# Attention scores in fp32 on four 32-row groups of TensorE, with the causal mask of the row maxima added on VectorE

## The reference

```python
q = jnp.einsum('btc,hcd->bhtd', x, Wq) + bq[None, :, None, :]     # 16 heads, D = 16
k = jnp.einsum('btc,hcd->bhtd', x, Wk) + bk[None, :, None, :]
v = jnp.einsum('btc,hcd->bhtd', x, Wv) + bv[None, :, None, :]
scores = jnp.einsum('bhtd,bhsd->bhts', q, k) * scale
causal = jnp.triu(jnp.full((Tn, Tn), neg, dtype=scores.dtype), k=1)
probs = jax.nn.softmax(scores + causal, axis=-1)
y = jnp.einsum('bhts,bhsd->bhtd', probs, v)
...
return y @ Wo + bo
# layer 1: no biases, q = _apply_rope(q, sin, cos), k = _apply_rope(k, sin, cos)
```

## Time and profile before

| | |
|---|---|
| time, median of 3 runs | 1030.9 us (1030.26 to 1034.15) |
| span of the profiled execution | 1058.4 us |
| PE busy | 754.7 us (71%) |
| DVE busy | 494.6 us (47%) |
| ACT busy | 330.7 us (31%) |
| POOL busy | 336.4 us (32%) |
| mean granted TensorE clock | 0.863 |

### The profile page before, as it was taken

How to read it: one execution, slowest core, us unless ns; L and a number is a source line. 1 busy time by engine, 2 the same in 40 slices (tenths; PEclk the granted TensorE clock), 3 DMA queues, 4 the chain that set the end, 5 groups by cost and what they waited for, 6 DMA issues and landing times.

```text
span 1058.4 us, 14617 instructions
## 1 busy us (share of the span) xinstructions
PE 754.7 (71%) x4353; PEld 439.7 (42%) x4353; DVE 494.6 (47%) x1442; ACT 330.7 (31%) x660; POOL 336.4 (32%) x371
## 2 busy tenths in 40 slices
PE   0930899996753889999881632589998496899970
PEld 0510334423521667666660321134434443576650
DVE  7211977804630344444444762587742740144444
ACT  1500366682200222222220340246674320032221
POOL 6210011120075255555457150001110047035560
PEclk9965899999575899999995776799999598899995
DMA  2599053480052799999997099300000111089974
GB/s 74 60 115 103 2 167 103 147 264 1 1 177 77 227 246 261 270 260 262 247 231 212 2 118 119 40 12 2 2 1 22 67 48 41 24 235 264 263 178 129
DMA packets 88634, 134.28 MB, mean 127 GB/s; under 512 B 9883, under 2 KB 67082, under 8 KB 88464
## 3 DMA queue, kind: packets, MB, share of 16 engines
q1 hardware_dynamic: 57808, 101.31, 38.0%
q0 software_dynamic: 16896, 19.37, 10.6%
q10 hardware_dynamic: 13888, 13.06, 4.4%
HBM read 80.74 MB, written 40.06 MB: 114 GB/s over the span
## 4 chain that ended last, share of the span: by engine, by line
PE 29%; DVE 18%; POOL 14%; issue 14%; DMA 11%; another core or an unknown queue 5%; SPq 4%; ACT 4%; POOLq 0%; ACTq 0%; DVEq 0%
POOL acc L578 12%; DVE mx L1134 7%; DMA KA<-X 6%; PE ps L703 5%; PE ps L687 5%; PE ps L764 4%; SPq L410 4%; PE ps L658 4%; DMA acc<-X,token 3%; PE ps L798 2%; PE ps L605 2%; POOL pause L576 2%; ACT X L922 1%; PE ps L732 1%
## 5 line engine op out<-in xcount | busy, mean ns | idle before, releaser
L1134 DVE TENSOR_REDUCE mx<-ps 128x1 f32<-128x512 f32 (+3 forms) x304 | 180.2, 657 | 128.1 <-PE ps L661 76.7
L658 PE MATMUL ps<-KA,QA 112*128 112x512 bf16 (+3 forms) x384 | 116.7, 355 | 85.6 <-ACT mT L941 44.1
L922 ACT ACTIVATE X<-ps 128x1024 f32<-128x1024 f32 (+1 forms) x192 | 146.2, 811 | 84.9 <-PE ps L687 84.3
L578 POOL DMA_INDIRECT acc<-X,token x96 | 149.8, 1561 | 15.1 <-issue 14.9
L821 PE MATMUL ps<-X,KA 128*128 128x128 f32 x1152 | 149.3, 280 | 1.4 <-DMA KA<-in_ex 0.8
L821 PEld LDWEIGHTS ps<-X,KA 128*128 128x128 f32 x1152 | 139.6, 196 | 4.3 <-issue 2.9
L555 POOL TENSOR_SCALAR_AFFINE_SELECT X<-X 128x512 f32<-128x512 f32 x64 | 40.8, 637 | 311.2 <-ACT X L922 311.2
L1337 DVE TENSOR_SCALAR X<-ps,egate 128x256 f32<-128x256 f32 x96 | 46.5, 484 | 145.5 <-DMA acc<-X,token 145.0
L566 POOL DMA_INDIRECT slot_rows<-xn,slot_i x64 | 64.8, 1013 | 127.2 <-issue 73.7
L658 PEld LDWEIGHTS ps<-KA,QA 112*128 112x128 bf16 x384 | 37.4, 103 | 157.4 <-DVE mx L1134 50.8
L990 ACT ACTIVATE X<-ps 128x256 f32<-128x256 f32 x96 | 36.9, 385 | 201.9 <-DVE token L1311 84.2
(11 more groups left out here) (174 smaller groups left out, 934.3 us busy)
## 6 DMA issues: line engine op xcount, KB each, us to landing
KA<-in_ex SPq DMA_DIRECT2D x96, 512.0 KB
slot_rows<-empty SPq DMA_DIRECT2D x12, 1060.0 KB, 10.1
X<-slot_rows ACTq DMA_DIRECT2D x96, 132.5 KB
QA<-X SPq DMA_DIRECT2D x28, 256.0 KB, 23.1
KA<-X SPq DMA_DIRECT2D x28, 256.0 KB, 25.4
KA<-in_dn SPq DMA_DIRECT2D x64, 64.0 KB
X<-acc SPq DMA_DIRECT2D x8, 512.0 KB, 6.6
acc<-empty SPq DMA_DIRECT2D x2, 1152.0 KB, 10.4
```

What stands on the lines that cost most here:

```text
L578: pool.indirect_dma_start(out=acc[L][r % 2], out_offset=bass.IndirectOffsetOnAxis(ap=token[:, r:r + 1], axis=0), in_=erows[:, r % 2, :], i ...
L658: mm = pe.matmul(ps[:, bank, j * w:(j + 1) * w], QA[0:KQ, h, i * P:(i + 1) * P], KA[0:KQ, h, s0:s0 + w], start=True, stop=not diag)
L922: nc.scalar.activation(probs[:, st % PB, 2 * p:2 * p + 2, off:CH], ps[:, 4 + 2 * p:6 + 2 * p, off:CH], ACT.Exp, scale=SCALE).then_inc(S(f" ...
L1134: v.tensor_reduce(mx[:, part, i, h0:h0 + nh], ps[:, n % RB, 0:nh * w].rearrange("p (h w) -> p h w", h=nh), AX.X, ALU.max)\
```

## The change

Scores are made by fp32 matmuls from the queries and keys themselves. A head has 16 rows, and the four heads of a group lie in partitions 0, 32, 64 and 96 onwards, so each head's matmul uses another 32-row group of the array. Splits, row copies and the rows of ones go. The projection's columns are ordered so that one result holds eight heads, two in each 32 partitions. ACT copies the keys twice, with a 0/1 scale that leaves the even heads (`KT`) or the odd ones (`k_odd`), and a DVE shuffle by 16 partitions brings the odd heads down (L1113).

A maximum unit is now always one head (192 of them in a layer). Where it has no diagonal block, DVE reduces it as before (L1129). Where it has one (128 of the 192), one DVE instruction adds the mask from `mask_d` and takes the running result (L1137), and a second one, which the builder adds, writes the accumulator out. The negated maximum lands in `shifts`, is turned by fp32 transposes (L630), and DVE adds it into row 16 of each head in `QT` (L1145). A score matmul so has 17 rows.

Values and the second half of the projections move in between the first units (`vpair`, `proj`), and RoPE is done in eight pieces of 512 columns. `schedule()` is new: a pair of units (two heads) after each half of the scores, on the two row groups which that half doesn't use, and one more pair every second step. All units are used up in step 32 of 48. `KA` no longer shares memory with the expert weights. Loads that stood between the row copies are issued at the start.

```diff
-def max_units():
...
+def max_units(c):
+    out = []
+    for i in range(TPC * c, TPC * (c + 1)):
+        out += [(i, s0, CH) for s0 in range(0, CH * c, CH)] + [(i, CH * c, (i % TPC + 1) * P)]
+    return out
 RB = 3
 PB = 3
-OWN_RATE, NEXT_RATE = 4, (5, 4, 4, 4)
+AHEAD = 6
+EXTRA = 2
...
     for st in range(last + 2):
         g, s = divmod(st, NSTEP)
...
+        if st < last and s in (0, TPC):
+            take_rows(NC * g + (s == TPC) + 1)
         for p in range(2):
             if st < last:
                 out.append(("score", st, p))
-            out += more[:1]
-            more = more[1:]
+            take(1 - p)
         if st >= 2:
             out.append(("weigh", st - 2))
...
+        if st % EXTRA == 0:
+            take_behind()
+        take_rows()
...
# SP
-                sp.wait_ge(S(f"k_ones{L}"), 1)
-                for m in range(KD):
-                    for part in range(PARTS):
-                        for j, (dst, those) in enumerate(((QA, Q_PARTS), (KA, K_PARTS))):
...
-                                    sp.dma_start(dst[DH * r:DH * (r + 1), HM * m:HM * (m + 1), :],
-                                                 parts[:, j, m, part, :]).then_inc(S(f"qa_rows{L}_{m}"), 16)
...
# GpSimd
+            ch.step(pool.memset(V[:, :, :, DH + 1:], 0.0))
...
-                pool.memset(KA[ONES_AT:KX, :, :], 1.0).then_inc(S(f"k_ones{L}"), 1)
...
# TensorE, unit(x)
-                            mm = pe.matmul(ps[:, bank, j * w:(j + 1) * w], QA[0:KQ, h, i * P:(i + 1) * P],
-                                           KA[0:KQ, h, s0:s0 + w], start=True, stop=not diag)
-                            if diag:
-                                mm = pe.matmul(ps[:, bank, (j + 1) * w - P:(j + 1) * w], identb[:, :], mask_q[:, :],
-                                               start=False, stop=True)
+                        _, g, i, h, s0, w = x
+                        at = slice(32 * h, 32 * h + DH)
+                        mm = pe.matmul(ps[:, bank, 0:w], QT[at, g, i * P:(i + 1) * P], KT[at, g, s0:s0 + w],
+                                       start=True, stop=True)
...
# TensorE, scores(st, p)
-                        mm = pe.matmul(ps[:, 4 + 2 * p + x, off:CH], KA[0:KX, h, b * P:(b + 1) * P],
-                                       QA[0:KX, h, c * CH + off:(c + 1) * CH], start=True, stop=True)
+                        at = slice(32 * (2 * p + x), 32 * (2 * p + x) + KS)
+                        mm = pe.matmul(ps[:, 4 + 2 * p + x, off:CH], KT[at, g, b * P:(b + 1) * P],
+                                       QT[at, g, c * CH + off:(c + 1) * CH], start=True, stop=True)
...
# ScalarE, head(x), layer 0
+                        for odd, dst in enumerate((KT[:, 2 * m, t], k_odd[:, NC * m + c, :])):
+                            nc.scalar.activation(dst, ps[:, bank, :], ACT.Identity, bias=k_bias[:, odd, m:m + 1],
+                                                 scale=half[:, odd:odd + 1]).then_inc(S(f"head_sb{L}"), 1)
...
# VectorE
+                            v.tensor_reduce(mx[:, i, h:h + 1], ps[:, bank, 0:w], AX.X, ALU.max, negate=True)\
+                             .then_inc(S(f"unit_out{L}"), 1)
...
+                            v.tensor_tensor_reduce(
+                                out=masked_s[:, d % 2, 0:w], in0=ps[:, bank, 0:w], in1=mask_d[:, CH - w:CH], scale=-1.0,
+                                scalar=mx[:, i, h:h + 1] if s0 else BIG, op0=ALU.add, op1=ALU.min,
+                                accum_out=shifts[:, i // TPC, i % TPC, 32 * h + SHIFT_ROW:32 * h + SHIFT_ROW + 1])\
+                             .then_inc(S(f"unit_out{L}"), 1)
+                    elif x[0] == "rows":
+                        _, g, c = x
+                        q = QT[:, g, c * CH:(c + 1) * CH]
+                        v.scalar_tensor_tensor(q, q, half[:, 0:1], ps[:, bank, :], ALU.mult, ALU.add)\
+                         .then_inc(S(f"unit_out{L}"), 1)
```

More of the change, by code:

```diff
@@ L79 @@
 NSTEP = len(STEPS)
-def max_units():
[L85 to L97, removed]
+NPROJ = 2 * KD * NC
+NVP = NT // 2
@@ L98, with proj, head_items @@
+def proj(u):
+    return u // (2 * NC), u // 2 % NC, u % 2
+def head_items():
+    out = [("proj", u) for u in range(2 * NC)]
+    rest = [("vpair", j) for j in range(NVP)] + [("proj", u) for u in range(2 * NC, NPROJ)]
+    return out, rest
+def max_units(c):
[3 more added lines that the diff above has]
+    return out
 RB = 3
 PB = 3
-OWN_RATE, NEXT_RATE = 4, (5, 4, 4, 4)
-OWN_AHEAD, NEXT_AHEAD = 10, 10
@@ L120, in schedule @@
         g, s = divmod(st, NSTEP)
[L121 to L141, removed]
+        if st < 4:
+            out.append(("rope", 4 + st))
+        if st in (1, 3):
+            out.append(("kmask", 3 + st))
+        if st in (4, 5):
+            out.extend(("shuf", u) for u in ((5, 4) if st == 4 else (7, 6)))
+        if st < last and s in (0, TPC):
+            take_rows(NC * g + (s == TPC) + 1)
         for p in range(2):
@@ L218, in S @@
             return sems[name]
[L220 to L227, removed]
-                              mT[HG * j:HG * (j + 1), c * CH:(c + 1) * CH]).then_inc(S(f"max_rows{L}_{c}"), 16)
-        def take_part(eng, L, m, j, part):
-            eng.wait_ge(S(f"parts_p{part}_{L}"), 2 * m + j + 1)
-            q = qkf[:, j, m, :]
-            eng.tensor_tensor(q if part == 1 else parts[:, j, m, 2, :], q, parts[:, j, m, part - 1, :], ALU.subtract)\
-               .then_inc(left(L, m, j, part)[0], 1)
         def sb(name, shape, dt=F32):
@@ L488, in _ @@
                               allow_small_or_imprecise_dtypes=True))
-            for t in (identf, identb, mask_q):
-                ch.step(pool.memset(t[:, :], 0.0))
+            for t in (identf, mask_d, shifts):
+                ch.step(pool.memset(t[:], 0.0))
             for t in (before, ones, ones_row):
@@ L934, in _ @@
                         exps(*x[1:])
[L935 to L945 removed]
+                    elif x[0] in ("proj", "vpair"):
+                        head(x)
+                    elif x[0] == "kmask" and L == 1:
+                        k_halves(x[1])
                     elif x[0] == "weigh":
@@ L1094, in xT_copy @@
                     v.tensor_copy(xT[:, k, CH:T], ps[:, KD + k, :]).then_inc(S("xT_dve"), 1)
+            for odd in range(2):
+                ch.step(v.memset(half[:, odd:odd + 1], float(odd)))
+            ch.wait()
+            for odd in range(2):
+                for x in range(HG):
+                    v.memset(half[32 * x:32 * x + DH, odd:odd + 1], float(1 - odd)).then_inc(S("half"), 1)
             halves = (list(range(0, TPC)), list(range(TPC, NT)))
```

425 lines of the change are left out of this document (219 added, 206 removed).

## The result

The changed kernel takes 1223.7 us (median of 4 runs) beside 1031.4 us for the kernel before: ratio 1.182, 95% interval 1.173 to 1.191. It is slower, and 216 us above the 1008 us forecast. One of the four runs was a slow one, of 1238.1 us: the ratio goes by the other three, whose median is 1218.8 us.

What follows compares the result with a forecast made beforehand. The steps were taken as bounded by PE with DVE close behind. Gains of 12 (start), 10 (layer 0) and 2 us (layer 1) made 24 of 1058.4, ratio 0.977, some 1008 us in timed runs; range 975 to 1062 us.

Steps and rivals of the forecast that it cites:

- PE's work hardly changes: Scores and units in a layer: 61 us of PE in fp32 row groups, where bf16 took 62 and the masks 7.
- 42.8: Layer 0: scores start 42.8 us after the first projection.
- 127 us: Layer 0, steps 0 to 32 with the other 164 units: 127 us, 1.2 times DVE's work.
- 32.4 us: Layer 0, steps 33 to 47 without units: 28.9 us, plus 3.5 for the end, 32.4 us.
- a lack of overlap: Rival: row groups don't overlap at all in score and unit matmuls; over 1250 us, chance 0.03.
- Two steps 7.1 us for ten units: Steps 0 to 32: an ordinary step takes 2.9 us, one with an extra pair 4.2; 33 steps 117 us.
- Row groups at the price of one: Score and unit matmuls: four row groups side by side cost as one head, 61 us a layer.
- program order: Rival: a head's two instructions hold back the next head, 38 us a layer; 1081 us, chance 0.10.
- Start of the program: Without the memset of `KA`, everything after the start comes some 12.0 us earlier.
- DVE's durations: Maximum units on DVE: masked ones 0.35 to 0.75 us, accumulator write 0.13; units 110 us in a layer.
- half-rate rival: Rival: DVE's masked unit reads at half the rate, 25 us more a layer; 1057 us, chance 0.10.
- Layer 1: Layer 1's attention: as layer 0 with RoPE in pieces, 212 against 214 us, 2 us gained.

Runs made afterwards that it cites:

- e1: The changed kernel with unit and score matmuls contracting over 32 rows in place of 16 and 17; 1071.8 us beside 1034.9 for the kernel before.
- e2: The changed kernel with unit and score matmuls over 64 rows, output not the reference's; 1114.0 us beside 1034.9 for the kernel before.
- e9: e1 with K's rows 17 to 31 of each group zero in place of ones; 1098.7 us beside 1061.0 for the kernel before.
- e16: e1 with every unit's reduction reading one column of its bank, maxima left out as work; 992.1 us beside 1033.4 for the kernel before.
- e5: e1 with the units in one bf16 pass; 1021.1 us beside 1058.1 for the kernel before.
- e6: The kernel before with GpSimd's memset of the ones rows of K waiting for layer 0's eight normalized tiles; ratio 0.991.
- e3: The changed kernel with a 128-row bf16 matmul added ahead of each pair's first unit; 1421.5 us beside 1034.9 for the kernel before.
- e12: e5 with no extra pairs of units, timed against the kernel before; ratio 0.954.

## Why the prediction was wrong

- **"PE's work hardly changes"** is the step that failed. It took every matmul at 0.43 us, a price from rows at full clock, and I never asked whether the clock would hold. It was 1.00 in the steps of before with 114 rows in a matmul, and 0.51 with 16 and 17. That the rows named decide most of it is shown by e1, e2 and e9, which change nothing in the order of the instructions: layer 0's attention goes from 310 to 239 us in e1. The clock slowed the weighing too, "21" us in steps 0 to 32. In layer 0 the first scores started 46.3 us after the first projection, for "42.8", and their first exponential 48.4 us after it. Steps 0 to 32, "127 us", took 214 from exponential to exponential; the last part, "32.4 us", took 47.6. These three make the 310.3 us. No rival held the clock either: the dearest that I priced was a lack of overlap, over 1250 us, which is another reason.
- **With 32 rows** (e1) those three are 48.4, 153 and 37.1 us, the first third of the steps still at half clock. So a second, smaller error stands behind the clock: what a pair loses when its bank is late. I had "Two steps 7.1 us for ten units" with that loss included, 32 us for nine steps. It is 37.1 with it, and 32.0 only when it is gone (e16). With the units' columns also cut (e5) the three are 41.0, 128.5 and 35.6 us, near my sizes, but that is luck and no confirmation: TensorE has a quarter of the unit columns there that I had priced, and 72 us at half clock.
- **Row groups at the price of one** was right where four are ready: four starts within 20 ns, and so again in the second round. But only 21% of the instructions found three others to start with, and my sum took all at a quarter of the price. The rival of **program order** (1081 us) is refuted by the same rows: the second unit's first instruction starts before the first unit's second. The rule of the Trainium skill that it was set beside, "TensorE: Matmul & The Clock Gate", section "The mechanism", that matmuls are never reordered, the trace contradicts there too.
- **Start of the program**, "12.0 us earlier": 12.0 measured (28.46 to 16.45 us), and e6 alone gives 11 in the kernel before.
- **DVE's durations** were right, the sum a little dear. The rows of the masked unit and of its accumulator's write:

```profile
L1129 DVE TENSOR_REDUCE mx<-ps 128x1 f32<-128x512 f32 x128 | 84.5, 688 | 90.7 <-PE ps L624 90.6
L1137 DVE CUSTOM_DVE_ANT_0 X<-ps,mask_d,mx 128x512 f32<-128x512 f32 x32 | 22.7, 748 | 25.8 <-PE ps L624 25.8
L1137 DVE CUSTOM_DVE_ANT_0 X<-ps,mask_d 128x512 f32<-128x512 f32 x32 | 21.3, 689 | 25.7 <-PE ps L624 25.7
L1137 DVE DVE_READ_ACCUMULATOR2_ANT shifts<- 128x1 f32 x256 | 21.3, 83 | 0.0
```

  0.69 us for 512 columns with the mask, 0.75 with the running result as well, 0.083 for the accumulator where I had 0.13. Back to back such a unit of 512 without a running result starts every 0.62 us (48.53 and 49.15 us in the timeline), where I had 0.75. The half-rate rival (1057 us) would have shown some 1.2 us. But DVE waits for TensorE 91 us in the first row alone: it was never "80% busy in steps 0 to 32", but 47% (102 of 218 us).
- **Layer 1**: RoPE was to cost 10 us more than layer 0. It is 3.7.

What stays open: why the clock is at half from 54 to 112 us in e1 and full after it with instructions of the same kinds (shorter waits for banks shorten it, e16), and why the full-array filler of e3 didn't lift it.

## What to carry to other kernels

Before work is moved into small tiles of the array, ask what TensorE's clock will be, not only how many columns there are: a busy engine can run at half speed, and the clock row of the page, beside a PE row of nines, is where it shows. If a matmul needs few rows, let it name all rows of its group, with zeros or with something that cancels; in this kernel that added no instruction and no column and gave 72 and 74 us in the two layers. And a maximum that softmax only needs roughly can be made in one bf16 pass. Together with an even spread of the units this gives the version of e12, 0.954 of the kernel before.

## What the runs showed of the hardware that I had not expected

- The clock was granted at half for 218 and 239 us on end with TensorE busy for 98% of them. The Trainium skill, "TensorE: Matmul & The Clock Gate", section "Why this matters for your kernels", advises to keep the engine busy, so that the clock stays up. The trace disagrees for matmuls of 16 and 17 rows, all fp32 (0.50 and 0.52 in the two windows) or with units in bf16 (0.54 to 0.61).
- It went with the rows named: 256 and 264 us at half in the two attentions with 16 and 17 rows, 65 and 63 with 32 (75 and 67 when 15 of them multiplied by zero), 0 and 8 with 64.
- A full-array bf16 matmul in every pair of units left it at 0.51, and 358 us of each attention at half.
- TensorE's busy share says nothing of its width: 99% both where pairs went alone (37.1 us) and where they lay side by side (32.0 us).
- A GpSimd memset of 13.75 us over 18 partitions held two DVE instructions on four columns in SBUF for 12.6 us; moved 9.5 us later (e6) it didn't lengthen the two copies out of PSUM that lay under it (0.69 us each), and the two instructions took 0.17 and 0.16 us.
